# Reordering the last groups of a projection stage: earlier spills of transposed rows, an earlier row sum, a scaling shared by two engines, and edge masks spread over four turns

## What is computed

```python
h = relu(_batchnorm(x @ W1.T + b1, g1, be1))
out = h @ W2.T + b2                      # "output stage" below
out = _batchnorm(out, g2, be2)
x = _layernorm(x + out, axis=-1)         # rows of x2
Xq = (x @ W_lin.T)                       # queries
Xv = (x @ W_val.T)                       # values
...
m = segment_max(e_t, src); ex = exp(e_t - m[src]); denom = segment_sum(ex, src)
```

## Time and profile before

| what | us |
|---|---|
| median of 3 runs | 1866.47 (1864.74 to 1866.65) |
| the profiled execution | 1867.78 |
| its span in the profile | 1866.0 |
| PE busy in the span | 1796.2 (96%) |
| DVE, ACT, POOL busy | 1465.6, 1101.3, 578.2 |

### The profile page before, as it was taken

The page is one execution under the profiler, slowest core; times in us unless marked ns, Lnnn a source line. Parts: engine busy times, 40 slices in busy tenths (PEclk is TensorE's granted clock), DMA queues, the critical chain, the costliest instruction groups (busy, mean ns, idle before and its releaser), DMA issues. The chain is left out here.

```text
span 1866.0 us, 35420 instructions
## 1 busy us (share of the span) xinstructions
PE 1796.2 (96%) x13191; PEld 1465.2 (79%) x13191; DVE 1465.6 (79%) x3952; ACT 1101.3 (59%) x1765; POOL 578.2 (31%) x1625
## 2 busy tenths in 40 slices
PE   7999999999999999999999999999899899999997
PEld 6777878888899999988887778876678544588875
DVE  7888875666666767878888879988777688798776
ACT  5555565455454555544444437767667699666676
POOL 3454521232323443000000004456554200104655
PEclk9999999999999999999999999999999899999999
DMA  4112000001000000010000024313222210003223
GB/s 136 29 35 69 1 24 23 1 1 46 1 2 1 1 1 1 1 46 1 1 1 1 1 66 145 115 46 91 79 80 77 93 46 23 12 1 104 81 79 105
DMA packets 63416, 77.75 MB, mean 42 GB/s; under 512 B 3974, under 2 KB 55436, under 8 KB 63244
## 3 DMA queue, kind: packets, MB, share of 16 engines
q1 hardware_dynamic: 62380, 72.35, 12.1%
q0 software_dynamic: 864, 3.15, 0.5%
HBM read 47.17 MB, written 28.31 MB: 40 GB/s over the span
## 5 line engine op out<-in xcount | busy, mean ns | idle before, releaser
L2205 ACT ACTIVATE l_gates<-l_acc,l_b 128x512 f32<-128x512 f32 (+1 forms) x408 | 240.0, 620 | 84.4 <-PE l_acc L480 82.6
L478 PE MATMUL l_acc<-l_x_hi,l_w1x_hi 128*128 128x336 f32 (+1 forms) x544 | 188.4, 346 | 1.0 <-ACT l_gates L2205 0.8
L480 PE MATMUL l_acc<-l_x_lo,l_w1x_hi 128*128 128x336 f32 (+1 forms) x544 | 187.5, 345 | 0.0
L479 PE MATMUL l_acc<-l_x_hi,l_w1x_lo 128*128 128x336 f32 (+1 forms) x544 | 187.2, 344 | 0.0
L2094 ACT ACTIVATE l_x_hi<-hT 128x512 fp32r<-128x512 f32 (+1 forms) x112 | 82.4, 786 | 173.6 <-PE l_acc L480 173.6
L478 PE MATMUL l_acc<-l_x_hi,l_w0x_hi 128*128 128x512 f32 x464 | 181.5, 391 | 3.3 <-ACT l_gates L2205 3.3
L480 PE MATMUL l_acc<-l_x_lo,l_w0x_hi 128*128 128x512 f32 x464 | 180.6, 389 | 0.0
L479 PE MATMUL l_acc<-l_x_hi,l_w0x_lo 128*128 128x512 f32 x464 | 180.6, 389 | 0.0
L2215 ACT ACTIVATE l_gates<-l_cell 128x512 f32<-128x512 f32 (+1 forms) x112 | 63.7, 569 | 168.5 <-DVE l_cell L2266 138.9
L249 POOL TENSOR_TENSOR bi_shifted<-bi_shifted 32x126 f32<-32x126 f32 (+61 forms) x62 | 18.0, 290 | 390.7 <-DVE bi_shifted L236 390.7
L478 PE MATMUL l_acc<-l_h_hi,l_w0h_hi 128*128 128x512 f32 x320 | 124.8, 390 | 0.7 <-DVE l_h_lo L2283 0.7
(11 more groups left out here) (547 smaller groups left out, 5374.0 us busy)
## 6 DMA issues: line engine op xcount, KB each, us to landing
xin<-in_x_t SPq DMA_DIRECT2D x16, 512.0 KB, 3.7
hidB<-in_x SPq DMA_DIRECT2D x16, 512.0 KB, 4.8
x<-hT SPq DMA_DIRECT2D x16, 512.0 KB, 3.2
hidB<-x SPq DMA_DIRECT2D x16, 512.0 KB, 3.8
x<-hidB SPq DMA_DIRECT2D x16, 512.0 KB, 2.9
attention_residual<-x SPq DMA_DIRECT2D x16, 512.0 KB, 3.9
out_x<-hT SPq DMA_DIRECT2D x16, 512.0 KB, 2.9
l_rawx<-in_wih SPq DMA_DIRECT2D x4, 1024.0 KB, 6.2
```

What stands on the lines that cost most here:

```text
L478: t.matmul(out, left[0], right[0], start=start, stop=False)
L479: t.matmul(out, left[1], right[0], start=False, stop=False)
L480: return t.matmul(out, left[0], right[1], start=False, stop=stop)
L2205: i = a.activation(gates[:, j, q, 0:n], acc[:, j, q, 0:n], FUNC[q], bias=b[:, o:o + 1])
```

## The change

The x2t pieces of group g - 1 are put into SP's queue ahead of the x2 store of group g, where before the pieces of group g - 2 stood behind it. In iteration 12 (g + 3 == LAST) DVE sums and measures group 15 before `xt_lo(13)`, and PE transposes group 15's output before `transposes_back(13)`. Group 15's rows are scaled half by ACT and half by DVE, as group 2's are; SP and PE wait for both. In the output stage `by_node` is copied in turn 2, and the four edge masks are made in turns 8 to 11, one in each.

```diff
+        BY_BOTH = {2: 2, LAST: 3}
...
             for g in range(GROUPS):
+                if g - 1 >= later.FIRST:
+                    put_rows_by(g - 1)
                 sp.wait_ge(n2.out, g + 2)
-                if g == 2:
-                    sp.wait_ge(bn_scaled, 2)
+                if g in BY_BOTH:
+                    sp.wait_ge(bn_scaled, BY_BOTH[g])
                 if g >= SEMS:
                     sp.wait_ge(stored2[g % SEMS], g // SEMS * 16)
                 sp.dma_start(x2v[g], rows(hidB, g)).then_inc(stored2[g % SEMS], 16)
-                if g - 2 >= later.FIRST:
-                    put_rows_by(g - 2)
-            put_rows_by(LAST - 1)
...
                     a.activation(m["gather"][:, :], ps_gather, ACT.Copy).then_inc(spread, 1)
+                if g == 2:
                     a.activation(by_node[:, :], ps_nodes, ACT.Copy).then_inc(by_node_done, 1)
...
-                    n2.scale(a, act, rows(hidB, g + 2), g + 2, range(TILES if g else TILES // 2))
+                    n2.scale(a, act, rows(hidB, g + 2), g + 2, range(TILES // 2 if g + 2 in BY_BOTH else TILES))
...
-                if g == 8:
-                    edge_masks(e)
+                if 8 <= g < 12:
+                    edge_mask(e, ("start", "last")[g % 4 // 2], g % 2 == 0)
                 pivot_steps(1)
...
+                if g + 3 == LAST:
+                    rows_out(LAST)
                 if g + 1 < GROUPS:
                     xt_lo(g + 1)
-                if g and g + 3 < GROUPS:
+                if g and g + 3 < LAST:
                     rows_out(g + 3)
+                if g + 2 == LAST:
+                    n2.scale_by_vector(v, dve, rows(hidB, LAST), LAST, range(TILES // 2, TILES), bn_scaled)
...
-                if g == 1:
+                if g in (1, LAST - 3):
                     transposes_of_output(g + 3)
                 if 1 <= g < LAST:
                     transposes_back(g + 1)
-                if 1 < g < GROUPS - 3:
+                if 1 < g < LAST - 3:
                     transposes_of_output(g + 3)
```

More of the change, by code:

```diff
@@ L1105, in edge_runs, with edge_mask @@
                 return e
[L1107 to L1110, removed]
+            def edge_mask(e, n, keep):
+                drop = m["drop_" + n][:, :]
+                if keep:
+                    e.after(v.tensor_scalar(m["keep_" + n][:, :], drop, -1.0, 1.0, ALU.mult, ALU.add))
+                else:
+                    e.after(v.tensor_scalar(drop, drop, -BIG, None, ALU.mult))
             def output_stats(g):
@@ L1314, in transposes_back @@
                 pe.wait_ge(n2.out, g + 2)
-                if g == 2:
-                    pe.wait_ge(bn_scaled, 2)
+                if g in BY_BOTH:
+                    pe.wait_ge(bn_scaled, BY_BOTH[g])
                 if g:
```

## The result

The changed kernel takes 1859.29 us (median of 5 runs, 1856.83 to 1859.77). The kernel before, run beside it, takes 1866.47 (5 runs, 1864.74 to 1867.56). The ratio is 0.9959, with a 95% interval of 0.9948 to 0.997. So it is faster by 0.4%, and more than the 0.2% that can be told from no change. The forecast was 1859.3.

The account below looks back on a forecast made before the run. PE is busy nearly everywhere, so only its standstill or half-clock time can be won. Median 1866.47 - 7.3 (query stage end) + 0 (output stage) + 0.1 (POOL's lag) = 1859.3 us; range 1857.5 to 1860.8, with two rivals up to 1862.3.

Parts of the forecast that it names:

- The end of the stage: End of the query stage: ACT's 4.74 wait gone, PE's pause at most 1.0, clock up; 7.3 us less.
- its bounds: Group 15's scaling in the query stage: DVE's half ends between 1455.8 and 1456.5.
- The output stage: Masks and `by_node` in the output stage: turn 9 starts 1.39 earlier, later given back; 0 in sum.
- A mask that meets POOL: Output stage, turns 8 and 10: a mask just behind a POOL subtraction's start costs 0.81.
- Both draws: Output stage, turns 9 and 11: mask and POOL's third subtraction start together; a mask that gets ahead costs 0.46.
- The rival that POOL wins the draws: Output stage: masks wait for POOL's third subtraction, 2.4 us slower, 1861.7; chance 0.24.
- The rival that the end hangs on a transfer: End of query stage: group 15's store lands late, ACT's last copy 0.9 to 3 late, 1860.2 to 1862.3; chance 0.12.
- the rival that it comes out slower: SP's in-order queue: group 15's store lands later than 1473.8, giving 1870 or more; chance 0.02.
- the clock in the next stage: Stage after the query stage: clock may stay up as PE's pause falls from 2.90 to about 1.8; counted as nothing.

Follow-up runs that it names:

- order alone: Kernel before with only SP's queue in the new order (pieces of g - 1 ahead of the store of g): 1863.56 us, ratio 0.9987.
- all but order: Changed kernel with SP's queue back in its old order (pieces of g - 2 behind the store of g): 1867.55 us, ratio 1.0001.
- late sum: Changed kernel with group 15's sum, statistics and PE transposes again behind the low half of group 13: 1860.73 us, ratio 0.9973.
- one engine scales: Changed kernel with ACT scaling all four tiles of group 15 and DVE none: 1859.72 us, ratio 0.996.
- the repeated profile: Profile of the changed kernel run once more, unedited: 1858.87 us, ratio 0.9956.
- the masks in POOL's gap: Changed kernel with the four masks behind the batch norm pass in turns 9 to 12: 1858.38 us, ratio 0.9957.
- the best: Changed kernel, masks behind the batch norm pass, next block's first operands built before `xt_lo(15)`, last query copy shared by ACT and DVE: 1858.06 us, ratio 0.9954.

## Why the prediction was right

| | before | order alone | all but order | late sum | one engine scales | changed |
|---|---|---|---|---|---|---|
| PE's pause ahead of `transposes_back(15)` | 4.69 | 3.36 | 4.44 | 2.62 | 1.17 | 0.67 |
| its eight transposes | 1.97 | 1.97 | 1.94 | 1.69 | 1.09 | 1.06 |
| query stage | 128.07 | 125.85 | 128.18 | 123.80 | 122.16 | 120.76 |

**The end of the stage.** Forecast 7.3 less, measured 7.31 (128.07 to 120.76). The steps hold one by one. `xt_hi(14)` started once PE had transposed; POOL's shift ended at 1454.36 (forecast 1454.7, and the program ran 0.25 ahead of before when the stage began); DVE's half took 1.11 beside POOL's two copies and ended at 1455.95, inside its bounds, and it is what PE waited for; PE's pause is under 1.0; from the transposes to the first product of group 15 took 3.74 (forecast 3.8). ACT and DVE end level, 0.4 ahead of the next block (0.55 was taken). The two experiments on the order of stores bear out that this wait had to go first: without it the rest gives nothing, and alone it gives 2.2 of 7.3. The parts don't add up (2.2 and -0.1 make 2.1, not 7.3), and the table shows why: the end of group 15's chain is the later of two branches, the landed pieces and POOL's shift, and the long pauses (2.62 and more) all ended in a slow clock, the short ones (0.67, 1.17) did not. How long a pause has to be can't be read from this: in the kernel before one of 2.04 left the clock at 1.00, and in the version with all but the store order one of 1.93 ahead of the next block was followed by a fall at 1475.9.

**The output stage.** Forecast 0, measured 0.07 longer. The earlier start of turn 9 came (PE at 1297.39 against 1299.08; less the 0.32 by which the whole program ran ahead at the stage's start, 1.37; forecast 1.39), and was given back: PE's first product of turn 11 stands at 1310.00, where 1310.25 less 0.32 was forecast, and by the tables above turns 9 to 12 start 1.37, 1.25 and 0.44 earlier and 0.14 later than before (forecast 1.39, 1.39 and 0.50 earlier, then level); DVE's last pass stands 0.05 behind. A mask that meets POOL was taken at 0.81, and cost 0.82 and 0.77. Both draws went to DVE. That POOL's third subtraction comes right behind its second, so that a waiting DVE instruction goes in between, is what I took for the reason. The rows don't show it: both have 1300.47 as their start, DVE 0.002 us ahead, and in the repeated profile POOL's record starts 0.013 ahead (1301.060 against 1301.073) and the mask took 0.40 all the same. So the size of a won draw is shown, and why DVE wins is not. The rival that POOL wins the draws fell. With the masks in POOL's gap the stage is 2.26 us shorter.

The Trainium skill (SBUF — State Buffer, "Who interferes with whom") has the first issuer keep the shared pair for the whole instruction while the other blocks. With that rule the trace agrees where the order is clear: 1.36 behind POOL, 0.42 in its gap. For the two level with POOL (0.40, and POOL's 1.56) the starts don't tell who issued first.

**The landings.** The rival that the end hangs on a transfer did not happen, but by 0.17 us only: the store of group 15 took 6.3, the forecast's longest was 6.4. So its chance of 0.12 was, if anything, set low. In the price of the rival that it comes out slower, the sum 1462.7 + 7.3 + 3.7 is 1473.7, not 1473.8; nothing hangs on it.

**What was not in the sum.** I counted nothing for the clock in the next stage. Before, it fell at 1471.7 for 3.4 us, behind the pause of 2.90; now, behind 1.64, it did not, and PE was 0.5 further ahead a few us into the next block. So the steps make 7.31 - 0.07 + 0.5 = 7.7, and the medians are 7.2 apart: within their spread. The profiled executions are 10.9 apart. Of the other 3.2, 0.32 stand ahead of the first stage that the change touches, and 2.9 far behind it. In the kernel before, the windows around two later pauses of PE had a clock of 0.83:

```profile
1620.00:1630.00 10.00, 8.05 (x36) 6.29 (x35) 7.98 (x18) 3.53 (x9) 4.67 (x5) 0.83 0.00 0
1755.00:1765.00 10.00, 7.42 (x158) 6.83 (x157) 5.45 (x10) 3.66 (x7) 6.73 (x27) 0.83 0.01 2
```

and in the changed kernel the same stretches had not:

```profile
1612.00:1622.00 10.00, 8.05 (x42) 6.15 (x41) 8.64 (x20) 4.55 (x12) 5.04 (x5) 1.00 0.00 0
1745.00:1755.00 10.00, 7.42 (x166) 6.69 (x166) 6.28 (x11) 4.57 (x8) 7.04 (x29) 1.00 0.01 2
```

Yet the pauses in them are equal, 1.37 and 2.26 us in either kernel. The forecast of the median was right to leave this out; but that its last tenth fits is luck, since the runs of one kernel spread over 3 us. Whether the change makes such falls rarer isn't settled. Neither the repeated profile of the changed kernel nor the one with the late sum has either of the two; the one in which ACT alone scales has the second (1754.6); and those with the masks moved, the best, the order alone and all but the order have the first. Most of these differ in when they get there, and other runs have no record of single falls.

## What to carry to other kernels

When a queue holds both a store that someone waits for and one that nobody needs yet, put each transfer where its consumer wants it, and look at what the freed engine waits for next: here the order of two kinds of DMA was worth 2.2 us alone and 7.3 with the next wait on the list shortened, while that one alone was worth nothing. A pause of TensorE is to be priced twice, by its length and by the slow clock that may follow it: here an edit of 1.6 us that brought it from 2.6 to 0.7 gave 3.0 in the profile. When a row names one engine and two feed the wait, look at which of the two ended last: here it was VectorE's half, and sharing the work gave 0.5 instead of 1.0. Small VectorE work was cheapest in a gap of GpSimd: find the gap in the timeline before you spread the work over turns (2.3 us of its stage here, though less of it reached the whole).

## What the runs showed of the hardware

- A VectorE tensor_scalar of 128x512 that takes 0.40 to 0.42 us by itself took 1.36 when it began 0.23 behind a GpSimd subtraction. When both began level (within 0.013 us, either one ahead), it took 0.40, and GpSimd's 1.56 to 1.58 instead of 1.30. This came out alike at both such places and in both profiles of the changed kernel.
- The same pause of TensorE is not always followed by the same clock. The one of 1.37 us (1616.08 in the changed kernel) was followed by a fall to a mean of 0.83 over 10 us in the kernel before and in the one with the masks moved, and by none in two profiles of the changed one. The one of 2.26 us was followed by a fall in two of the nine profiles. One such fall costs about 1 to 1.5 us, so two of them would be most of the spread between runs of one kernel. The first five of the changed kernel stand in two clusters, at 1856.8 to 1857.0 and 1859.3 to 1859.8; their mean granted clocks, 0.994 and 0.993 against 0.993, 0.992 and 0.991, fit that only loosely, and the five of the repeat (1857.5, 1857.6, 1858.9, 1859.0, 1859.9) don't cluster as clearly. That the spread is those falls is argued, not shown.
